# Local attention in a fused four-layer kernel: scores as four products of 32 partitions, keys zeroed four ways per chunk, rstd kept by token, units alternating between two pairs of PSUM banks

## The chip, the cores and the metric

The kernel runs on one NeuronCore of a Trainium2 chip. The metric is the device time in microseconds (us) of one execution. Matmuls of fp32 operands run as two records each in the trace; of fp32r operands as one.

## The reference, cut to what matters

The reference runs four layers over 2048 tokens of 128 channels (each an attention or scan part and a feed-forward part). The change touches the attention part of the second layer, L1:

```python
NUM_HEADS = 16; HEAD_DIM = 8; WINDOW = 64; SCALE = 8.0 / HEAD_DIM   # SCALE is 1
xw = x.reshape(B * nw, WINDOW, C)
qkv = (xw @ W_qkv).reshape(B * nw, WINDOW, 3, NUM_HEADS, HEAD_DIM)
q, k, v = (qkv[:, :, 0], qkv[:, :, 1], qkv[:, :, 2])
q = _layernorm(q, ln_gamma, ln_beta)        # over the 8 values of a head
k = _layernorm(k, ln_gamma, ln_beta)
attn = jnp.einsum('bqhd,bkhd->bhqk', q * SCALE, k)
attn = jax.nn.softmax(attn, axis=-1)
out = jnp.einsum('bhqk,bkhd->bqhd', attn, v).reshape(B * nw, WINDOW, C)
out = out @ W_proj + b_proj
```

## The kernel before, in words

The 2048 tokens are four chunks of 512 (`NC = 4`, `CH = 512`); a chunk is four tiles of 128. Each engine runs its own hand-written list of steps in order; semaphores tie the lists together. The stages follow each other over all chunks: a first stage, FFN0 (16 experts, 8 blocks a chunk), the local attention (`attn`), FFN1, a scan, FFN2, a linear attention, two dense blocks. While a stage works on chunk c, hooks (`attn_hooks`) prepare the normalised input of a later chunk or stage and add the result of the chunk before to the residual.

In the attention stage a chunk is eight units (`UN = 8`, 32 in all). Unit N is tile N // 2 and half of the heads, u = N % 2: eight heads, two windows of 64 tokens. Per unit: `scores` (L1219 to L1224) makes two products, one per window, of all 128 channels: 64 queries are loaded, 512 columns stream (8 heads x 64 keys); keys of one head must be zero in the channels of all others, so there is one masked copy of the keys per head. The result fills bank `G[u]`. DVE takes the maximum (L1395) and subtracts it into `PRB` (L1398); ACT takes the exponential in place (L1329); PE transposes four 128 x 128 blocks into bank `U[u]` (`turn`, L1232); ACT copies them to `PT` (`evac`, L1335); PE multiplies with the values (`weigh`, L1244); after every second unit DVE divides by the sums (`finish`, L1374, L1380), which must be done before the next tile's first `weigh`, as both use one bank.

The masked copies are made per tile, 16 of 128 x 128 (`attn_mask`, L1188 to L1204): 8 on DVE and 4 on POOL (L1203), 4 on ACT (L1201), in two buffers (`KM`).

During a chunk the q, k and v of the next are prepared in steps (`PREPARE_AT`, `attn_prepare_*`): step 0 and 1 are the products for q and k (three fp32r products of 512 columns, L731 to L733), their squares and copies (L1145, L1146); step 2 the means of the squares, 32 rows by 512 tokens (L1107, L1108), square root on ACT (L1149, between two table loads) and reciprocal on DVE (L1176); step 3 the values (L1155); step 4 spreads the reciprocals over the channels by products of 32 rows (L1119, L1125), and DVE multiplies (L1181) and applies gain and bias (L1185), for k and then q. For chunk 0 these steps lie in the last chunk of FFN0 (`attn_early_*`). The values are turned and placed in two halves (L1135, L1169). The output of a chunk is turned, copied, split and projected during the next one (`attn_turn_pe` L1296, `attn_out_act` L1308, `attn_project_*` L1302, L1313, L1319, L1321).

`body_start` makes PE, ACT, DVE and POOL wait, before the first masks and scores, for FFN0's last result (L926). POOL also converts weights (`work`, L2117, L2118).

## Time and profile before

| | |
|---|---|
| median of 3 runs | 897.65 us (897.23 to 898.66) |
| the profiled execution | 897.48 us, span 895.7 us |
| PE busy | 734.7 us (82%) |
| DVE busy | 675.6 us (75%) |
| ACT busy | 575.3 us (64%) |
| POOL busy | 394.1 us (44%) |
| mean granted PE clock | 0.911 |

Times in the trace count from the start of the span. [...]

### The profile page before, as it was taken

The numbers are of one execution on the slowest core, as the hardware profiler recorded it, in microseconds if no ns is written. First come the engines' busy times: TensorE is split into PE (matmuls) and PEld (weight loads), VectorE is DVE, ScalarE is ACT, GpSimd is POOL, SyncE is SP. The second block draws the span as 40 slices with busy tenths as digits, with TensorE's granted clock in tenths as the row PEclk, the third lists the DMA queues.
The fourth block names the chain that finished last, engine by engine and source line by source line (L and its number), as shares of the span: only waits on it lengthen the run. The fifth ranks groups of instructions, "written<-read, shape, count | busy, mean of one in ns | idle before, by whom it ended". The sixth has DMA issues, their size and how long they took to land. (4 is left out here: it accounts for less than half of the span.)

```text
span 895.7 us, 11019 instructions
## 1 busy us (share of the span) xinstructions
PE 734.7 (82%) x3306; PEld 467.0 (52%) x3306; DVE 675.6 (75%) x1615; ACT 575.3 (64%) x926; POOL 394.1 (44%) x427
## 2 busy tenths in 40 slices
PE   4778998779999889999678888867777767777787
PEld 3666765345545567777555666642232222222575
DVE  6685776798898748787756667769898788786785
ACT  4264664657474535565636667767899979777776
POOL 6638654634445015544248767634333332230330
PEclk9999998988696869999969999998999889789999
DMA  4200001000000000000000000000000000000001
GB/s 134 69 12 15 15 15 33 19 23 24 12 25 19 1 0 1 1 1 0 1 13 23 1 1 0 1 0 1 1 0 1 1 1 0 1 0 1 1 1 48
DMA packets 9610, 11.59 MB, mean 13 GB/s; under 512 B 720, under 2 KB 5712, under 8 KB 9552
## 3 DMA queue, kind: packets, MB, share of 16 engines
q1 hardware_dynamic: 9552, 10.89, 4.2%
q8 instruction: 27, 0.44, 0.2%
q14 instruction: 31, 0.25, 0.1%
HBM read 9.84 MB, written 1.05 MB: 12 GB/s over the span
## 5 line engine op out<-in xcount | busy, mean ns | idle before, releaser
L989 POOL TENSOR_TENSOR rbuf<-B,rbuf 128x512 fp32r<-128x512 f32 x126 | 164.2, 1307 | 101.8 <-ACT rbuf L921 101.0
L968 DVE TENSOR_TENSOR B<-B,spread_bank 128x512 f32<-128x512 f32 x128 | 87.1, 682 | 47.2 <-ACT B L913 33.0
L921 ACT ACTIVATE rbuf<-B 128x512 fp32r<-128x512 f32 x132 | 83.0, 628 | 49.0 <-PE y_bank L733 38.8
L497 POOL TENSOR_SCALAR small<-small 128x4 f32<-128x4 f32 x32 | 8.1, 252 | 175.9 <-DVE small L387 175.7
L731 PE MATMUL y_bank<-rbuf,WH 128*128 128x512 f32 x150 | 64.2, 428 | 20.8 <-POOL rbuf L989 14.4
L955 DVE TENSOR_TENSOR B<-B,up_banks 128x512 f32<-128x512 f32 x68 | 46.5, 684 | 45.4 <-PE up_banks L733 28.5
L911 ACT ACTIVATE B<-gate_banks 128x512 f32<-128x512 f32 x68 | 40.8, 599 | 61.6 <-PE gate_banks L733 60.4
L1715 ACT ACTIVATE B<-B,VEC 128x1024 f32<-128x1024 f32 x48 | 55.2, 1150 | 22.3 <-DVE B L1710 22.3
L731 PE MATMUL gate_banks<-XH,WH 128*128 128x512 f32 x152 | 66.7, 439 | 0.8 <-ACT YT L1313 0.8
L733 PE MATMUL gate_banks<-XH,WL 128*128 128x512 f32 x152 | 62.4, 411 | 0.0
L732 PE MATMUL gate_banks<-XL,WH 128*128 128x512 f32 x152 | 61.9, 407 | 0.0
L1203 POOL TENSOR_SCALAR B<-S,WR 128x128 f32<-128x128 f32 x64 | 39.2, 629 | 49.7 <-DVE S L1185 38.1
L733 PE MATMUL y_bank<-rbuf,WL 128*128 128x512 f32 x150 | 60.2, 402 | 0.0
L732 PE MATMUL y_bank<-rbuf,WH 128*128 128x512 f32 x150 | 60.0, 400 | 0.0
L1617 POOL TENSOR_SCALAR WH<-WK 128x512 fp32r<-128x512 f32 x22 | 13.8, 628 | 104.6 <-issue 57.9
L1244 PEld LDWEIGHTS spread_bank<-VB,B 128*128 128x128 f32 x256 | 37.6, 226 | 34.1 <-issue 26.2
L866 PE MATMUL spread_bank<-SCT,WE 128*128 128x512 f32 x96 | 42.6, 444 | 10.7 <-DVE B L968 8.7
L1716 ACT ACTIVATE B<-B 128x1024 f32<-128x1024 f32 x48 | 50.5, 1052 | 0.0
L913 ACT ACTIVATE B<-gate_banks,WR 128x512 f32<-128x512 f32 x64 | 43.8, 687 | 10.0 <-PE gate_banks L733 9.5
L731 PEld LDWEIGHTS y_bank<-rbuf,WH 128*128 128x128 f32 x150 | 28.9, 193 | 40.2 <-POOL rbuf L989 23.2
L1221 PE MATMUL gate_banks<-B,S 128*64 128x512 f32 x128 | 44.6, 786 | 5.3 <-issue 3.8
L1244 PE MATMUL spread_bank<-VB,B 128*128 128x36 f32 x256 | 41.1, 314 | 2.0 <-DVE Z L1380 2.0
(318 smaller groups left out, 2110.8 us busy)
## 6 DMA issues: line engine op xcount, KB each, us to landing
STG<-in_w_split SPq DMA_DIRECT2D x27, 256.0 KB, 2.7
X<-in_x SPq DMA_DIRECT2D x4, 256.0 KB, 4.6
out<-X SPq DMA_DIRECT2D x4, 256.0 KB, 2.3
WR<-in_w_raw SPq DMA_DIRECT2D x1, 524.5 KB, 4.0
STG<-in_w_exact SPq DMA_DIRECT2D x2, 256.0 KB, 2.7
STG<-in_w_split SPq DMA_DIRECT2D x5, 64.0 KB, 1.9
STG<-in_w_split SPq DMA_DIRECT2D x1, 192.0 KB, 2.3
STG<-in_w_split SPq DMA_DIRECT2D x1, 128.0 KB, 2.1
```

The costliest lines, as they stand in the source:

```text
L731: nc.tensor.matmul(dst, w[0], x[0], start=start, stop=False)
L732: nc.tensor.matmul(dst, w[0], x[1], start=False, stop=False)
L733: return nc.tensor.matmul(dst, w[1], x[0], start=False, stop=stop)
L913: nc.scalar.activation(AO[n % 2], G[n % 2][:, :], ACT.Relu, bias=raw("b1_2", b, 1))\
L921: nc.scalar.activation(rbuf[n % 2][:, :], HO[n % 3], ACT.Copy).then_inc(hh_ready, 1)
L955: nc.vector.tensor_tensor(MO[n % 2], AO[n % 2], U[n % 2][:, :], ALU.mult).then_inc(mul_done, 1)
L968: nc.vector.tensor_tensor(HO[n % 3], src, SP[:, :], ALU.mult).then_inc(h_ready, 1)
L989: e_.tensor_tensor(rbuf[2 + n % 2][:, :], HO[n % 3], rbuf[n % 2][:, :].bitcast(F32), ALU.subtract).then_inc(hl_ready, 1)
L1221: i = nc.tensor.matmul(G[u][w * WIN:(w + 1) * WIN, :], QN[c_ % 2][:, tok], KM[tile % 2][:, HU * u:HU * u + HU, w * WIN:(w + 1) * WIN], sta ...
L1244: i = nc.tensor.matmul(SP[:, pr * 36:(pr + 1) * 36], PT[u][:, q * P:(q + 1) * P], VB[:, tile % TL, pr, :, :, :].rearrange("p a b d -> p (a ...
L1715: nc.scalar.activation(CS[p % 4], AB[p % 4], ACT.Sin, scale=-TURN, bias=half_pi).then_inc(cos_ready, 1)
L1716: nc.scalar.activation(SN[p % 4], RB[p % 4], ACT.Sin, scale=-TURN).then_inc(sin_ready, 1)
```

## The change

Scores: each unit is now four products. The heads of a unit are four neighbours in one 32-partition group (`k` = 0, 1) and again four in the next; a product takes 32 partitions, 64 queries and 4 x 64 = 256 key columns, and writes 64 partitions of one of two banks (`SB2[u]`: the pair G for u = 0, the pair U for u = 1). Of keys only four copies a chunk are needed, head h mod 4 each, 128 x 512, with gain and bias applied in the same operation (`attn_keys`): two on ACT, two on POOL, none on DVE. The transposes of unit N go into the same pair of banks as its scores, so the scores of unit N + 2 wait for the copy (`evac`) of unit N, where they waited for the subtraction (L1398) before. On PE `weigh` comes before the scores, on ACT `evac` before the exponential, and `finish` one unit earlier on DVE.

Rstd by token: step 2 is eight products of 16 columns, with 128 tokens as rows; square root and reciprocal work on 128 x 128 instead of 32 x 512. ACT spreads them to 128 x 512 twice (`attn_spread_act`), and steps 4 and 5 turn them back on PE (four products of 128 columns each) into the routing bank, k and q at separate units. The first two units' scores are issued within FFN0's last blocks and `body_start` is gone; FFN0's last two down products now stand behind them on PE.

```diff
         def later_weights(g, chain):
+            for row, dst in (("ln_g1", key_g), ("ln_b1", key_b)):
+                i = nc.gpsimd.tensor_scalar(dst, raw("head_of_4"), raw(row), 1.0, ALU.mult, ALU.mult)
+            chain(i)
             WM32 = buf[11]
...
                 for at_ in lagged(f, c, b, f.lag):
                     down(*at_)
+                    if f is FFN0 and at_ == (NC - 1, f.blocks - 3):
+                        for N in range(2):
+                            attn_scores(pe, N)
...
+        KG = 4
         QN = [S0[:, 0:CH], S0[:, CH:2 * CH]]
-        KN = [S0[:, 2 * CH:3 * CH], S0[:, 3 * CH:4 * CH]]
         Zf = Z[:, :, :].rearrange("p a b -> p (a b)")
         AT = [Zf[:, 0:CH], Zf[:, CH:2 * CH]]
         qc, kc = Zf[:, 2 * CH:3 * CH], Zf[:, 3 * CH:4 * CH]
-        KM = [B[:, 4 * k_:4 * k_ + 4, :].rearrange("p a b -> p (a b)").rearrange("p (h t) -> p h t", h=NH)
-              for k_ in range(2)]
-        PRB = [buf[8], buf[9]]
-        PT = [buf[10], buf[11]]
+        KM = [B[:, 7:11, :], B[:, 3:7, :]]
+        PRB = [buf[0], buf[1]]
+        PT = [buf[2], buf[11]]
+        SB2 = [GG[:, :].rearrange("p (k x) -> p k x", k=2)[:, :, 0:KG * WIN],
+               UU[:, :].rearrange("p (k x) -> p k x", k=2)[:, :, 0:KG * WIN]]
         WK = sb("WK", [P, 3, CH])
         sqq, sqk = WK[:, 0, :], WK[:, 1, :]
-        sdev, rstd = WK[0:GR, 2, :], WK[0:GR, 0, :]
+        sdev, rstd = WK[:, 2, 0:TL * GR], WK[:, 2, TL * GR:2 * TL * GR]
         A32w = WK[:, 1, :]
...
-        PREPARE_AT = {1: 0, 2: 1, 3: 2, 5: 3}
+        PREPARE_AT = {0: (0,), 1: (1,), 2: (2,), 4: (4,), 5: (5, 3)}
+        EARLY_AT = {0: (0,), 1: (1,), 2: (2,), 4: (4,), 5: (5,), 6: (3,)}
...
+            if b == 3:
+                attn_spread_act(a, 0)
+            if b == 6:
+                attn_keys(nc.scalar, 0)
...
-                nc.tensor.matmul(R[0:GR, :], raw("mean_k"), sqk, start=True, stop=False)
-                nc.tensor.matmul(R[0:GR, :], raw("mean_q"), sqq, start=False, stop=True).then_inc(var_full, 1)
+                for j in range(TL):
+                    for sq, name, at_ in ((sqq, "mean_q", 0), (sqk, "mean_k", NH)):
+                        i = nc.tensor.matmul(R[:, j * GR + at_:j * GR + at_ + NH], sq[:, j * P:(j + 1) * P],
+                                             raw(name, at_, NH), start=True, stop=True)
+                i.then_inc(var_full, 1)
...
-            if step == 4:
-                if not c:
-                    pe.wait_ge(v_copied, 1)
-                pe.wait_ge(rstd_qk, c + 1)
-                nc.tensor.matmul(R[:, :], raw("spread_k")[0:GR, :], rstd, start=True, stop=True).then_inc(rstd_full, 1)
-            if step == (4 if c else 5):
-                if c:
-                    pe.wait_ge(v_copied, c + 1)
-                else:
-                    pe.wait_ge(qk_read, 1)
-                nc.tensor.matmul(VQ(c)[:, :], raw("spread_q")[0:GR, :], rstd, start=True, stop=True).then_inc(rstd_full, 1)
+            if step in (4, 5):
+                pe.wait_ge(rstd_wide, 2 * c + step - 3)
+                if step == 5:
+                    pe.wait_ge(qk_read, 2 * c + 1)
+                for j in range(TL):
+                    i = nc.tensor.matmul(R[:, j * P:(j + 1) * P], (sqq, QN[c % 2])[step - 4][:, j * P:(j + 1) * P],
+                                         ident, start=True, stop=True)
+                i.then_inc(rstd_full, 1)
...
+        def attn_spread_act(a, c):
+
+            a.wait_ge(rstd_qk, c + 1)
+            if c >= 2:
+                a.wait_ge(s_full, UN * (c - 1))
+            for dst, at_ in ((sqq, NH), (QN[c % 2], 0)):
+                nc.scalar.activation(dst.rearrange("p (t h d) -> p t h d", t=TL, d=HD),
+                                     bcast(rstd.rearrange("p (t h) -> p t h", t=TL)[:, :, at_:at_ + NH].unsqueeze(3),
+                                           [P, TL, NH, HD]), ACT.Copy).then_inc(rstd_wide, 1)
...
-            if step == 4:
-                for k, (bank_, x, dst) in enumerate(((R, kc, KN), (VQ(c), qc, QN))):
-                    v.wait_ge(rstd_full, 2 * c + k + 1)
-                    v.wait_ge(centred, 2 * c + 2)
-                    nc.vector.tensor_tensor(x, x, bank_[:, :], ALU.mult).then_inc(qk_read, 1)
-                    v.wait_ge(qk_read, 2 * c + k + 1)
-                    if c >= 2:
-                        v.wait_ge(s_full, UN * (c - 1))
-                    nc.vector.tensor_scalar(dst[c % 2], x, raw("ln_g1"), raw("ln_b1"), ALU.mult, ALU.add)\
-                        .then_inc(qk_ready, 1)
-
-        def attn_mask(eng, tile):
-
-            c, i_ = tile // TL, tile % TL
-            if tile >= NC * TL:
+            if step in (4, 5):
+                k, x = step - 4, (kc, qc)[step - 4]
+                v.wait_ge(rstd_full, 2 * c + k + 1)
+                v.wait_ge(centred, 2 * c + 2)
+                nc.vector.tensor_tensor(x, x, R[:, :], ALU.mult).then_inc(qk_read, 1)
+            if step == 5:
+                v.wait_ge(qk_read, 2 * c + 2)
+                if c >= 2:
+                    v.wait_ge(s_full, UN * (c - 1))
+                nc.vector.tensor_scalar(QN[c % 2], qc, raw("ln_g1"), raw("ln_b1"), ALU.mult, ALU.add)\
+                    .then_inc(qk_ready, 1)
+
+        def attn_keys(eng, c):
+            if c >= NC:
                 return
-            heads, done = {nc.vector: (range(0, 8), masked_dve), nc.gpsimd: (range(8, 12), masked_pool),
-                           nc.scalar: (range(12, 16), masked_act)}[eng]
-            eng.wait_ge(qk_ready, 2 * c + 1)
-            if tile >= 2:
-                eng.wait_ge(s_full, 2 * (tile - 2) + (1 if eng is nc.vector else 2))
-            for h in heads:
-                dst, src = KM[tile % 2][:, h, :], KN[c % 2][:, i_ * P:(i_ + 1) * P]
+            eng.wait_ge(qk_read, 2 * c + 1)
+            if c >= 2:
+                eng.wait_ge(s_full, UN * (c - 1))
+            elif c == 1:
+                eng.wait_ge(yt_ready, count(2, 0))
+            for j in ((0, 1) if eng is nc.scalar else (2, 3)):
+                dst = KM[c % 2][:, j, :]
                 if eng is nc.scalar:
-                    i = eng.activation(dst, src, ACT.Copy, scale=raw("head_mask", h, 1))
+                    i = eng.activation(dst, kc, ACT.Identity, scale=key_g[:, j:j + 1], bias=key_b[:, j:j + 1])
                 else:
-                    i = eng.tensor_scalar(dst, src, raw("head_mask", h, 1), None, ALU.mult)
-            i.then_inc(done, 1)
+                    i = eng.tensor_scalar(dst, kc, key_g[:, j:j + 1], key_b[:, j:j + 1], ALU.mult, ALU.add)
+            i.then_inc(keys_act if eng is nc.scalar else keys_pool, 1)
+
+        def attn_scores(pe, N):
+            if N >= NU:
+                return
+            u, c, i_ = N % 2, N // UN, N % UN // 2
+            if N % UN == 0:
+                pe.wait_ge(keys_act, c + 1)
+                pe.wait_ge(keys_pool, c + 1)
+                pe.wait_ge(qk_ready, c + 1)
+            if N >= 2:
+                pe.wait_ge(pt_ready, N - 1)
+            else:
+                pe.wait_ge(act_done, NC * FFN0.blocks)
+                pe.wait_ge(mul_done, NC * FFN0.blocks)
+            for w in range(2):
+                tok = slice(i_ * P + w * WIN, i_ * P + (w + 1) * WIN)
+                for k in range(2):
+                    rows = slice(32 * (2 * u + k), 32 * (2 * u + k) + 32)
+                    i = nc.tensor.matmul(SB2[u][w * WIN:(w + 1) * WIN, k, :], QN[c % 2][rows, tok],
+                                         KM[c % 2][rows, :, tok], start=True, stop=True)
+            i.then_inc(s_full, 1)
...
                 if N:
                     turn(N - 1)
-                scores(N + 1)
                 if N >= 2:
                     weigh(N - 2)
+                if N:
+                    attn_scores(pe, N + 1)
                 if n == 0:
                     attn_values_pe(pe, c, 1)
                     if c == 0:
                         hook(-1)
+                if nxt:
+                    for step in PREPARE_AT.get(n, ()):
+                        if step != 3:
+                            attn_prepare_pe(pe, c + 1, step)
                 if n == 3 and c:
                     attn_turn_pe(pe, c - 1)
                 if n == 4 and c:
                     attn_project_pe(pe, c - 1)
-                attn_hooks(n, c, hook, 4)
-                if n in PREPARE_AT and nxt:
-                    attn_prepare_pe(pe, c + 1, PREPARE_AT[n])
+                attn_hooks(n, c, hook, 5)
+                if nxt and n == 5:
+                    attn_prepare_pe(pe, c + 1, 3)
...
-            if c + 1 < NC:
-                pe.wait_ge(qk_read, 2 * c + 4)
+            if c + 2 < NC:
+                pe.wait_ge(centred, 2 * c + 5)
...
                 if N >= 2:
                     a.wait_ge(o_full, N - 1)
-                nc.scalar.activation(PT[N % 2], U[N % 2][:, :], ACT.Copy).then_inc(pt_ready, 1)
-
-            if c == 0:
-                body_start(a, 2, 0)
-                attn_mask(nc.scalar, 0)
+                else:
+                    a.wait_ge(h_ready, NC * FFN0.blocks)
+                nc.scalar.activation(PT[N % 2].rearrange("p (k x) -> p k x", k=2), SB2[N % 2], ACT.Copy)\
+                    .then_inc(pt_ready, 1)
+
             for n in range(UN):
                 N = c * UN + n
-                probs(N)
                 if N:
                     evac(N - 1)
-                if n == 1:
+                probs(N)
+                if n == 0:
                     attn_values_act(a, c, 1)
+                if nxt:
+                    for step in PREPARE_AT.get(n, ()):
+                        if step != 3:
+                            attn_prepare_act(a, c + 1, step)
+                if n == 3 and nxt:
+                    attn_spread_act(a, c + 1)
+                if n == 3 and c:
+                    attn_out_act(a, c - 1)
                 if n == 4 and c:
                     attn_project_act(a, c - 1)
                 attn_hooks(n, c, hook, 5)
-                if n in PREPARE_AT and nxt:
-                    attn_prepare_act(a, c + 1, PREPARE_AT[n])
-                if n == 3 and c:
-                    attn_out_act(a, c - 1)
-                if n % 2 == 0:
-                    attn_mask(nc.scalar, c * TL + n // 2 + 1)
+                if n == 5 and nxt:
+                    attn_keys(nc.scalar, c + 1)
+                if n == 6 and nxt:
+                    attn_prepare_act(a, c + 1, 3)
...
-                Sv = G[u][:, :].rearrange("p (h k) -> p h k", k=WIN)
-                chain(nc.vector.tensor_reduce(amax[:, HU * u:HU * u + HU], Sv, AX.X, ALU.max))
+                Sv = SB2[u].rearrange("p k (h x) -> p k h x", x=WIN)
+                amax_ = amax[:, HU * u:HU * u + HU].rearrange("p (k h) -> p k h", k=2)
+                chain(nc.vector.tensor_reduce(amax_, Sv, AX.X, ALU.max))
                 if N >= 2:
                     v.wait_ge(p_turned, N - 1)
-                nc.vector.tensor_tensor(PRB[u].rearrange("p (h k) -> p h k", k=WIN), Sv,
-                                        bcast(amax[:, HU * u:HU * u + HU].unsqueeze(2), [P, HU, WIN]), ALU.subtract)\
-                    .then_inc(s_read, 1)
-                if n == 6 and nxt:
+                nc.vector.tensor_tensor(PRB[u].rearrange("p (k h x) -> p k h x", k=2, x=WIN), Sv,
+                                        bcast(amax_.unsqueeze(3), [P, 2, KG, WIN]), ALU.subtract).then_inc(s_read, 1)
+                if nxt and n == 3:
+                    attn_prepare_dve(v, c + 1, 2)
+                if nxt and n == 4:
                     attn_prepare_dve(v, c + 1, 4)
-                if u == 0:
-                    if N >= 4:
-                        finish(N // 2 - 2)
-                    attn_mask(nc.vector, N // 2 + 1)
+                if nxt and n == 5:
+                    attn_prepare_dve(v, c + 1, 5)
                 if n == 4 and c:
                     attn_project_dve(v, c - 1)
                 if n == 0 and c == 0:
                     hook(-1)
-                attn_hooks(n, c, hook, 7)
-                if n == 5 and nxt:
-                    attn_prepare_dve(v, c + 1, 2)
+                attn_hooks(n, c, hook, 6)
+                if u == 1 and N >= 3:
+                    finish(N // 2 - 1)
...
-                body_start(g, 2, 0)
-                attn_mask(nc.gpsimd, 0)
+                attn_keys(nc.gpsimd, 0)
             for n in range(UN):
-                if n % 2 == 0:
-                    attn_mask(nc.gpsimd, c * TL + n // 2 + 1)
+                if n == 5:
+                    attn_keys(nc.gpsimd, c + 1)
                 attn_hooks(n, c, hook, 4)
                 if n % 2 and n > 1:
                     work()
```

## Rows read from the trace of the kernel before

**Rows 1.** The page: its first line.
```profile
span 895.7 us, 11019 instructions
```

**Rows 2.** Windows, a chunk each: us, busy PE, PEld, DVE, ACT, POOL, granted clock, DMA.
```profile
163.80:197.10 33.30, 27.01 (x130) 13.46 (x127) 31.78 (x80) 20.40 (x49) 17.40 (x28) 0.91 0.09 24
197.10:236.80 39.70, 38.81 (x169) 22.23 (x169) 33.95 (x94) 24.19 (x62) 16.76 (x24) 0.76 0.08 21
236.80:274.10 37.30, 36.14 (x169) 20.63 (x169) 34.87 (x94) 23.72 (x61) 16.61 (x24) 0.82 0.07 18
274.10:321.30 47.20, 38.23 (x199) 26.14 (x199) 32.20 (x116) 22.36 (x56) 7.77 (x12) 0.75 0.02 7
```

**Rows 3.** Timeline of PE in chunk 2: start, us, operation.
```profile
247.09 1.08 PE L1221 MATMUL gate_banks<-B,S 128*64 128x512 f32 x4
248.10 1.08 PE L1244 MATMUL spread_bank<-VB,B 128*128 128x36 f32 x8
249.01 0.48 PE L731 MATMUL route_bank<-XH,WH 128*128 128x512 f32 x1
...
249.80 0.60 PE L1232 MATMUL up_banks<-WR,B 128*128 128x128 f32 x4
```

**Rows 4.** The same, 22 us later.
```profile
271.02 1.09 PE L1232 MATMUL up_banks<-WR,B 128*128 128x128 f32 x4
272.08 1.98 PE L1221 MATMUL gate_banks<-B,S 128*64 128x512 f32 x4
```

**Rows 5.** Groups of instructions, 163.8 to 321.3 us: count, busy us, mean ns, idle before.
```profile
L1203 POOL TENSOR_SCALAR B<-S,WR 128x128 f32<-128x128 f32 x60 | 36.5, 625 | 44.0 <-DVE S L1185 38.1 <-PE gate_banks L1221 5.9
L1203 DVE TENSOR_SCALAR B<-S,WR 128x128 f32<-128x128 f32 x120 | 30.8, 333 | 0.4
...
L1395 DVE TENSOR_REDUCE small<-gate_banks 128x8 f32<-128x512 f32 x32 | 21.8, 682 | 11.5 <-PE gate_banks L1221 11.1
L1329 ACT ACTIVATE B<-B 128x512 f32<-128x512 f32 x32 | 20.1, 629 | 32.2 <-DVE B L1398 31.8
L1201 ACT ACTIVATE B<-S,WR 128x128 f32<-128x128 f32 x60 | 19.0, 390 | 0.0
L1335 ACT ACTIVATE B<-up_banks 128x512 f32<-128x512 f32 x32 | 18.8, 586 | 8.2 <-PE up_banks L1232 8.1
...
L1380 DVE TENSOR_TENSOR Z<-spread_bank,small 64x64 f32<-64x64 f32 x64 | 11.4, 218 | 0.8
L1176 DVE RECIPROCAL WK<-WK 32x512 f32<-32x512 f32 x3 | 10.0, 3330 | 0.0
L1374 DVE RECIPROCAL small<-spread_bank 64x16 f32<-64x16 f32 x32 | 8.1, 252 | 5.3 <-PE spread_bank L1244 5.1
L1169 ACT ACTIVATE VB<-route_bank 64x64 f32<-64x64 f32 x56 | 7.8, 218 | 10.4 <-PE route_bank L1135 6.9 <-PE spread_bank L1244 3.5
...
L2117 POOL TENSOR_SCALAR WH<-STG 128x512 fp32r<-128x512 f32 x9 | 5.6, 621 | 0.0
...
L1149 ACT ACT_TABLE_LOAD x3 | 3.8, 1283 | 0.1
...
L1185 DVE TENSOR_SCALAR S<-Z,WR 128x512 f32<-128x512 f32 x6 | 3.3, 547 | 0.2
...
L1308 ACT ACTIVATE WK<-y_bank 128x512 f32<-128x512 f32 x4 | 2.3, 582 | 5.9 <-PE y_bank L1296 5.9
```

**Rows 6.** Timeline, the step from FFN0 to attention.
```profile
154.43 0.46 POOL L2118 TENSOR_TENSOR WL<-STG,WH 128x128 fp32r<-128x128 f32 x1
...
158.00 0.60 PE L1135 MATMUL route_bank<-WR,KVT 128*128 128x128 f32 x4
...
162.41 3.07 PE L1221 MATMUL gate_banks<-B,S 128*64 128x512 f32 x8 [3.82 <-issue]
...
165.27 0.63 ACT L1329 ACTIVATE B<-B 128x512 f32<-128x512 f32 x1 [2.19 <-DVE B L1398]
```

**Rows 7.** The chain that ended last, in the linear attention: start, us, what.
```profile
782.05 0.99 PE spread_bank L1656 x8
```

More of the change, by code:

```diff
@@ L1087, in attn_early_dve @@
                 attn_prepare_dve(v, 0, 2)
-            if b == 6:
-                attn_prepare_dve(v, 0, 4)
+            for step in (4, 5):
+                if step in EARLY_AT.get(b, ()):
+                    attn_prepare_dve(v, 0, step)
         def attn_prepare_pe(pe, c, step):
@@ L1143, in attn_prepare_act @@
                 if c and step == 0:
[L1144 removed]
+                    a.wait_ge(qk_ready, c)
+                if c and step == 1:
+                    a.wait_ge(keys_pool, c)
                 nc.scalar.activation(sq, src[:, :], ACT.Square)
```

56 lines of the change are left out of this document (16 added, 40 removed).

## The prediction

> **What bounds it now.** I read the windows by chunk first. The span is 895.7 us [rows 1]; the attention stage, from the first maximum to FFN1's first product, is the four stretches of [rows 2], 157.5 us. In chunks 1 and 2 PE is busy for 38.81 of 39.70 and 36.14 of 37.30 us, DVE for 33.95 and 34.87: PE carries the chunk and DVE is close behind. ACT (24 us) and POOL (17 us) have room. The timeline of PE gives the second half of the answer. At the high clock the scores of a unit take 1.01 us start to start, weighing 0.91, one fp32r triple 0.79, and four transposes about 0.55 [rows 3]. In the same chunk, 22 us later, the same transposes last 1.09 and the same scores 1.98 [rows 4]: the clock is at its lower level. The mean clocks of 0.76 and 0.82 [rows 2] say how long: (1 - 0.76) x 2 x 39.7 = 19 us of chunk 1, 13 us of chunk 2. PE's work at the high clock is 8 x (0.55 + 1.01 + 0.91) = 19.8, four triples 3.2, and some 6 us of means, spreads and turns: 29 us. Half of 13 us on top makes 35.5 of the 37.3. So a chunk costs PE's work, the half-clock stretch, and one or two us of waits. DVE's masks and its reciprocal of 3.33 us are what PE waits for when it waits [rows 5].
>
> **The change, part by part.**
> *Masks.* 120 operations of DVE (30.8 us), 60 of POOL (36.5) and 60 of ACT (19.0) go [rows 5]. What comes per chunk is two operations of 128x512 on ACT (the nearest row is the copy, 0.58) and two on POOL (0.62) [rows 5]. One gain-and-bias operation of DVE (0.55) goes too. DVE loses about 8 us a chunk, ACT nets 5 - 1.2.
> *Rstd.* The reciprocal streams 128 columns instead of 512. Between 3330 ns for 512 and 252 ns for 16 [rows 5], a line gives 0.95 us: -2.4 on DVE. ACT gains two spreads of 128x512, 1.2 us. On PE the means become 16 records; weighing has 8 of such loads in 0.91 [rows 3], so 1.8 us, and the turns of steps 4 and 5 are 0.9 each: together 3.6, as before.
> *Scores.* No row shows products of different partition groups side by side. Upper bound: they share the array only by window, as now; then 256 columns twice cost the present 1.01. Lower bound: all four overlap. Four products of 512 columns in four column groups take 0.99 [rows 7], so half the columns take 0.5. I take 0.55, since that row is the nearest in kind (four small tiles at once). PE saves 0.45 a unit, 3.7 a chunk; with 1.01 it would save nothing.
> [...]
>
> *New waits.* This is the dear part. Scores of unit N + 2 now stand behind `evac` of N, and ACT does much else. I lay out chunk 1 at the high clock, 0 being the end of its first scores; durations as above, exp 0.63, evac 0.59, a DVE pass 0.69 [rows 5], placing values 8 x 0.14 = 1.1 (the row's 218 ns are overlapped ends).
> - Scores 2 end at 3.0: PE has turned and weighed at 2.0, but ACT places values and only then copies.
> - Scores 3 at 7.0: placing and the squares and copies of q (2.2 us on ACT) hold evac to 6.4.
> - Scores 4 at 10.2: the k product and its square and copy.
> - Scores 5 at 14.0: PE does the means (1.8), then transposes and weighs.
> - Scores 6 at 18.6: ACT waits for the means, changes tables twice (1.28 each, [rows 5]), does the exponential, waits for the reciprocal, spreads twice, copies the output (0.58) and the next input, and reaches evac at 17.4. PE is idle for 1.5 us.
> - Scores 7 at 24.1: DVE stands before step 4 until PE has issued it behind scores 6 (19.5), then multiplies, splits the output and the input (2 us), and only at 22.4 takes the next maximum. The projection waits for the split, 1.9 us of PE.
> - Scores 8 at 29.1: step 5, the tail's turn and the v product are 2.2 us of PE; DVE's multiply, gain and `finish` (0.5 + 0.8) hold weighing to 27.6.
> - The next chunk's first scores at 31.9.
> PE's work is 25.4 us of these 31.9. The chain scores, two DVE passes, exp, turn, evac alone is 4.2 us for two units, so it does not bind; the side work on ACT and DVE does.
>
> *The clock.* Before the fall in chunk 2 PE was busy but partly with products that fill a quarter of the array (means, spreads: 32 rows or columns). The spreads now fill it, but scores fill it for half the time, and the stretch from scores 4 to scores 7 has 3 to 4 us of idle PE. I therefore keep a half-clock stretch of about 14 us a chunk, over the scores 4 to 7. There PE's share is 8 to 9 us of high-clock work, of which most is on the path: +7.5 a chunk. [...]
>
> *The sum.* Chunks 1 and 2: 31.9 + 7.5 = 39.4 each, against 39.7 and 37.3. Chunk 0 has no output of a chunk before it: 29.1 + 5.5 = 34.6 against 33.3. The last chunk has no preparation; the same layout gives 33.2 from its first scores to FFN1's first product, +7 for the clock, 40.2 against 47.2 [rows 2], because PE no longer waits for masks there.
> *Start.* Masks and scores stood between the last value turn at 158.0 and the first exponential at 165.27 [rows 6]. Now the scores are done inside FFN0's end, but they need POOL's two key copies, and POOL is busy until 154.9 [rows 6]: 156.2, so they hold FFN0's last two down products by about 1.5 us, and with these the values and ACT's result. The exponential follows at some 163: it counts as a start at 160.8 instead of 163.8, -3.
> In FFN0's last chunk DVE saves the same 2.4 us of reciprocal; -1.5 of it reaches PE (0 to -2.4), ACT's extra 2.4 us lie in its idle time.
> Total: -3 - 1.5 + 1.3 - 0.3 + 2.1 - 7.0 = -8.4 us. The profiled execution took 897.48 for its span of 895.7, 0.17 below the median of 897.65; 897.5 - 8.4 = **889.1**. SP's queue keeps its order, and POOL, which loses 36.5 us of masks, has the weights ready earlier: 0.
>
> **The rivals.**
> *A: the clock stays high.* For it: less waiting for masks, and steps 4 and 5 fill the array. Then the 27.5 us of clock cost in my sum go: -36; with half of them gone, -22, **875**. Against it: each of the first three chunks lost the clock in its second half [rows 2, 4] though PE was busy there.
> *B: the half-clock stretch grows (slower).* The loop scores, evac, scores keeps PE waiting in every slot, and short 32-row scores keep the array emptier. If the stretch goes from 14 to 28 us in each chunk, PE's 25 us of work lie almost wholly in it: +7.5 in three chunks and about +3 in the last, 889.1 + 25 = **914**. It decides from where the clock costs 9 instead of the 7 us a chunk of my sum, which is only some 4 us more at the low level; a mild form, +12 us, gives 901. By itself, scores at 1.01 would add some 8 us where PE is on the path: 897.
> *C: no change.* The expected gain is only in the last chunk and at the start; if the layout is 2 us too short per chunk it is gone: **897.5**. That the change does not do what it says I exclude: the masks leave the lists.
>
> **How the numbers follow.** A measurement of this kernel tells about 0.2%, 1.8 us, from no change. My forecast (a gain of 2 to 16 us) gets 0.43, A 0.24, B 0.25, C 0.08. Faster 0.67, same 0.08, slower 0.25. The likeliest case alone spans 881 to 896. Reaching half into A and into the mild form of B, the range is 868 to 905: the clock term is the unknown that makes it this wide.
>
> **What would show it.** Right: no L1203 or L1201; DVE busy 22 to 25 us a chunk; a reciprocal near 0.95; scores of a unit in about 0.55 start to start; chunk 0 near 34, chunks 1 and 2 near 39, and the last near 40 us; DVE idle for about 4 us ahead of step 4; ACT as the releaser of scores in the first slots; a mean clock near 0.8 in each chunk. Wrong: a mean clock over 0.9 (A) or under 0.65 (B), scores at 1.0, or chunks under 33 us at the present clock, which would mean that ACT and DVE get through their side work without holding the loop.

## The result: 914.5 us, slower, and the profile after

The changed kernel takes 914.52 us (median of 4 runs, 909.35 to 918.38), the kernel before, on the same chip, 898.15 (897.23 to 898.83): a ratio of 1.0186, 95% interval 1.0154 to 1.0218. The forecast was 889.1 with a range of 868 to 905; rival B gave 914. Medians here and below are of all executions; three of the four of late_swap_fill ran at 929.3 to 930.3 us and one at 914.93, and one of rstd_mask_7 ran at 930.29 and one of true_64 at 901.39, over 1.5% above the fastest of their kernel; the ratios leave these slow ones out.

The windows by chunk of the changed kernel, beside [rows 2] (first maximum of the chunk to that of the next; the last ends at FFN1's first product; columns as there: length, busy time of PE, its loads, DVE, ACT and POOL, then the granted clock):

```profile
158.10:198.80 40.70, 36.36 (x200) 29.00 (x198) 21.64 (x53) 21.86 (x47) 7.73 (x10) 0.63 0.08 20
198.80:243.70 44.90, 39.14 (x230) 31.98 (x229) 24.23 (x62) 21.44 (x49) 9.52 (x10) 0.64 0.07 18
243.70:290.10 46.40, 39.77 (x222) 32.30 (x221) 24.17 (x62) 21.53 (x48) 9.50 (x10) 0.63 0.05 15
290.10:340.10 50.00, 42.79 (x219) 35.08 (x217) 25.69 (x86) 18.19 (x42) 3.08 (x4) 0.53 0.02 6
```

DVE fell from 34 to 24 us a chunk as forecast, and the chunks still grew, from 39.7 and 37.3 to 44.9 and 46.4 us. Cut into windows of 0.5 us, the trace shows two levels of the granted clock: from 150 to 345 us 296 of 390 windows read 0.50 and 79 read 1.00, the other 15 lie between (in the kernel before, from 150 to 325 us, 139 of 350 read 0.50, 197 read 1.00 and 14 lie between). So the clock is at the lower level for (1 - 0.64) x 2 x 44.9 = 32 us of chunk 1 and 34 of chunk 2, against 19 and 13 before. PE's busy time rose, from 38.8 and 36.1 to 39.1 and 39.8 us, though its work shrank, because the work is stretched by the clock (weighing a unit lasts 0.98 us at the high clock and 1.76 at half clock, below). Nearly all of the loss lies in this stage: FFN1's first product starts at 340.07 against 321.28, and what follows takes 576.3 us against 574.4.

The groups of the changed operations (158 to 340 us; line, engine, names, shapes, count, then busy time and mean ns, then idle time ahead of them):

```profile
L1250 PE MATMUL gate_banks<-B,S 32*64 32x256 f32 x123 | 16.4, 610 | 9.1 <-ACT B L1367 9.0
...
L1124 PE MATMUL route_bank<-WR,WK 128*128 128x16 f32 x48 | 8.0, 312 | 0.0
...
L1230 POOL TENSOR_SCALAR B<-Z,small 128x512 f32<-128x512 f32 x6 | 6.6, 1111 | 61.0 <-DVE Z L1208 61.0
...
L1228 ACT ACTIVATE B<-Z,small 128x512 f32<-128x512 f32 x6 | 4.5, 801 | 0.0
...
L1208 DVE TENSOR_TENSOR Z<-Z,route_bank 128x512 f32<-128x512 f32 x6 | 4.1, 688 | 25.6 <-PE route_bank L1138 25.6
...
L1203 DVE RECIPROCAL WK<-WK 128x128 f32<-128x128 f32 x3 | 2.9, 953 | 4.6 <-ACT WK L1166 4.6
```

The reciprocal takes 0.953 us (forecast 0.95); DVE idles 25.6 us in six ahead of steps 4 and 5, 4.3 each (forecast 4, for step 4); ACT's `evac` is what scores wait for, 9.0 us in the even units. The keys were dearer: 0.80 us each on ACT and 1.11 on POOL, for which I had taken a copy's 0.58 and 0.62.

PE's timeline around the chunk's start, the one longer stretch at the high clock (238.3 to 252.0 us; start, duration from first start to last end, and in brackets the idle time before):

```profile
241.35 0.98 PE L1272 MATMUL spread_bank<-VB,B 128*128 128x36 f32 x8
242.41 0.66 PE L1250 MATMUL gate_banks<-B,S 32*64 32x256 f32 x8
243.00 0.66 PE L1150 MATMUL route_bank<-WR,KVT 128*128 128x128 f32 x4
...
247.71 0.98 PE L1272 MATMUL spread_bank<-VB,B 128*128 128x36 f32 x8
251.59 0.82 PE L1250 MATMUL gate_banks<-B,S 32*64 32x256 f32 x8 [2.90 <-ACT B L1367]
252.34 0.80 PE L736 MATMUL route_bank<-XH,WH 128*128 128x512 f32 x1
...
254.63 1.76 PE L1272 MATMUL spread_bank<-VB,B 128*128 128x36 f32 x8
```

A unit's scores take 243.00 - 242.41 = 0.59 us from start to start (forecast 0.55; the duration of 0.66 runs 0.07 past the next start), where the same number of products of all 128 rows takes 1.02 (rows_128, from 263.58 to 264.60), and four products of 128 columns on all rows and columns, with half as many columns in all, take 0.99 (rows_128, L1138, from 280.01 to 281.00): four products of different row and column groups do run side by side. Weighing is 0.98 before 252.0 and 1.76 after it; the granted clock is 1.00 from 238.3 to 252.0 and 0.50 from 252.0 to 266.0. The clock falls here right behind a wait of 2.90 us, in which PE's third scores stand behind `evac`, and ACT places values before it.

The head of the stage, which was to gain 3 us (PE, then ACT and POOL):

```profile
151.17 0.50 PE L871 MATMUL spread_bank<-SCT,WE 128*128 128x512 f32 x1 [2.74 <-DVE B L976]
...
156.89 0.70 PE L1250 MATMUL gate_banks<-B,S 32*64 32x256 f32 x4 [3.83 <-issue]
...
158.07 0.80 PE L736 MATMUL y_bank<-rbuf,WH 128*128 128x512 f32 x1
...
160.80 1.05 PE L1150 MATMUL route_bank<-WR,KVT 128*128 128x128 f32 x4
...
147.80 1.51 ACT L1228 ACTIVATE B<-Z,small 128x512 f32<-128x512 f32 x2
149.21 0.59 ACT L919 ACTIVATE B<-gate_banks 128x512 f32<-128x512 f32 x1
...
165.04 0.63 ACT L1359 ACTIVATE B<-B 128x512 f32<-128x512 f32 x1
...
155.28 1.51 POOL L1230 TENSOR_SCALAR B<-Z,small 128x512 f32<-128x512 f32 x2
```

ACT copies keys ahead of FFN0's last silu (L919), and PE waits 2.74 us (1.35 in late_scores, where the copies stand behind it, though the product itself starts no earlier there, at 151.18); then it waits 3.83 us for POOL's keys inside FFN0, in front of the last two down products, which start at 158.07 at half clock (0.80). The first exponential is at 165.04, before it was at 165.27 [rows 6].

### The profile page after: what moved, and what is told of

The parts are those of the page before. It is cut to its first block and busy times, and to the rows that moved or that the text cites. A ratio compares the mean times of both kernels' runs of the same rounds, so it can differ in the third digit from the quotient of the medians.

```text
span 916.4 us, 11149 instructions
## 1 busy us (share of the span) xinstructions
PE 750.6 (82%) x3530; PEld 514.4 (56%) x3530; DVE 636.3 (69%) x1483; ACT 565.1 (62%) x878; POOL 365.2 (40%) x373
## 5 line engine op out<-in xcount | busy, mean ns | idle before, releaser
L963 DVE TENSOR_TENSOR B<-B,up_banks 128x512 f32<-128x512 f32 x68 | 46.5, 684 | 46.0 <-PE up_banks L738 25.4
L919 ACT ACTIVATE B<-gate_banks 128x512 f32<-128x512 f32 x68 | 40.6, 598 | 59.5 <-PE gate_banks L738 58.3
L736 PEld LDWEIGHTS y_bank<-rbuf,WH 128*128 128x128 f32 x150 | 29.1, 194 | 43.4 <-POOL rbuf L997 23.8
L1272 PEld LDWEIGHTS spread_bank<-VB,B 128*128 128x128 f32 x256 | 50.9, 295 | 3.3 <-issue 1.8
L1272 PE MATMUL spread_bank<-VB,B 128*128 128x36 f32 x256 | 49.7, 358 | 2.3 <-DVE Z L1416 2.2
L2149 POOL TENSOR_TENSOR WL<-STG,WH 128x512 fp32r<-128x512 f32 (+3 forms) x34 | 40.8, 1200 | 2.8
L1729 DVE TENSOR_SCALAR B<-gate_banks 128x1024 f32<-128x1024 f32 x32 | 38.9, 1215 | 2.2 <-PE gate_banks L1671 1.2
```

The costliest lines, as they stand in the source:

```text
L736: nc.tensor.matmul(dst, w[0], x[0], start=start, stop=False)
L963: nc.vector.tensor_tensor(MO[n % 2], AO[n % 2], U[n % 2][:, :], ALU.mult).then_inc(mul_done, 1)
L1272: i = nc.tensor.matmul(SP[:, pr * 36:(pr + 1) * 36], PT[u][:, q * P:(q + 1) * P], VB[:, tile % TL, pr, :, :, :].rearrange("p a b d -> p (a ...
```

## The experiments

All are measured against the kernel before on the same chip in the same job; each job had its own median of before, 898.1 to 899.5. The four lengths run from the first maximum of a chunk to that of the next, the last to the last maximum. Half clock is (1 - clock) x 2 x length, summed over the four, in the one execution of each kernel that was profiled (for late_swap_fill there is no interval). rows_128, rows_64 and before_rows_32 compute another attention than the reference.

| kernel | median us | ratio to before, 95% | chunks 0, 1, 2, 3 | half clock of all |
|---|---|---|---|---|
| before | 898.15 | 1 | 33.3, 39.7, 37.3, 33.3 | 50 of 144 |
| after | 914.52 | 1.0154 to 1.0218 | 40.7, 44.9, 46.4, 35.5 | 129 of 167 |
| fill_after | 917.59 | 1.0154 to 1.0268 | 46.0, 42.5, 45.4, 37.8 | 93 of 172 |
| rows_128 | 915.12 | 1.0114 to 1.0231 | 44.4, 46.5, 38.8, 34.0 | 69 of 164 |
| late_scores | 909.86 | 1.0068 to 1.0201 | 35.7, 49.5, 43.6, 30.6 | 111 of 159 |
| fill_before | 896.54 | 0.9949 to 1.0023 | 34.7, 40.9, 40.8, 34.1 | 38 of 150 |
| late_fill | 921.03 | 1.0210 to 1.0334 | 37.5, 49.9, 53.2, 40.2 | 86 of 181 |
| late_swap | 905.22 | 1.0042 to 1.0107 | 35.5, 44.4, 44.2, 35.2 | 120 of 159 |
| late_swap_fill | 929.53 | - | - | - |
| rstd_alone | 895.01 | 0.9936 to 0.9993 | 32.6, 38.9, 37.5, 35.8 | 40 of 145 |
| rows_64 | 891.31 | 0.9897 to 0.9945 | 31.8, 41.5, 37.1, 31.4 | 77 of 142 |
| before_rows_32 | 937.77 | 1.0401 to 1.0476 | 36.9, 48.6, 48.6, 43.5 | 143 of 178 |
| scores_alone | 909.73 | 1.0067 to 1.0156 | 38.4, 44.2, 44.0, 31.9 | 115 of 158 |
| rstd_mask_7 | 922.57 | 1.0176 to 1.0312 | 42.1, 38.6, 49.7, 33.2 | 77 of 164 |
| true_64 | 898.01 | 0.9947 to 1.0005 | 34.3, 42.5, 40.8, 34.2 | 99 of 152 |
| true_64_order | 892.64 | 0.9923 to 0.9963 | 38.8, 38.1, 37.6, 31.7 | 89 of 146 |

### Does the clock cost the time? Fillers and fuller products

```diff
# fill_after, in turn (before its wait for the exponential) and after an even unit's weighing
+        def fill(n, dst):
+            for _ in range(n):
+                nc.tensor.matmul(dst, wh("wqk1c")[0], WH[:, 0:224], start=True, stop=True)
...
+                pe.wait_ge(s_read, N + 1)
+                fill(4 if N else 12, SB2[u][:, 0, 0:224])
                 pe.wait_ge(p_ready, N + 1)
...
+                if u == 0:
+                    fill(4, SP[:, 288:CH])
```

> The changed kernel with idle-time products of TensorE added in the attention stage: four of 128x224 (fp32r, nothing reads them) while TensorE waits for each unit's exponential, four after every even unit's weighing, 24 in the wait for POOL's keys at FFN0's end. They add about 45 us of busy time at half clock, half of it at the high clock. Theory T (the changed kernel is slow because its emptier array loses the high clock for nearly the whole stage): the clock stays high in most of the stage, the chunks come near the 32 us of my layout, and the time falls by 15 to 35 us to 880 to 900. Rival R (scores behind evac and the side work on ACT and DVE set the chunks whatever the clock): the clock may rise, but the time stays within 4 us of 914 or goes above it.

The fillers raised the clock only in part (93 of 172 us at half clock, from 129 of 167), and each costs PE 0.13 us at the high and 0.25 us at half clock (four take 0.53 us from 204.92 to 205.45 and 0.98 from 182.95 to 183.93); in the timeline PE mostly goes from them to its next work with no idle time between, so that they lay on the path. The time is the one that R named and not T's, but with the fillers on the path it doesn't tell the two apart. (24 more fillers stand ahead of the first scores.) fill_before puts the same fillers into the units of the kernel before:

> The kernel before with the same idle-time products: four of 128x224 ahead of each unit's turn while the exponential is awaited, four after every even unit's weighing. Its attention stage has 62 us at half clock in 157.5. Theory T: most of that goes, the chunks are bound by VectorE's 34 us and by waits, 880 to 892. If the clock were worth little there (R): 897 to 905, the added products on the path.

No clear difference from before, and neither T's 880 to 892 nor quite R's 897 to 905. That clock gained and fillers paid cancel is my reading, not shown apart. late_fill and late_swap_fill, with more of them, were worse than the kernels that they were added to (late_swap_fill's best execution, 914.93, is above all of late_swap's), and T's numbers for them were wrong; late_fill's 921.0 is the case of a clock that stays low, 915 to 925, which decides nothing:

> late_scores with more idle-time products: six of 128x224 while each exponential is awaited, eight after every even unit's weighing, twelve ahead of the third scores, eight ahead of each projection. The first filled kernel kept half clock for 30.7 us of chunk 0 and for 93 of 172 us in all, and its fillers lay on the path there. Theory T: late_scores is at 909.9; if the clock now stays high for over two thirds of the stage, the chunks take about 33.5 us plus 2 to 3 us of fillers (that is what the chunks of the changed kernel and of late_scores give when their half-clock time is taken out at 0.37 us each), and the time is 888 to 900. Rival R: over 905 although the clock is high. If the clock stays low the run decides nothing: 915 to 925.

> late_fill and late_swap together. Theory T: at the high clock waits are what is left, so that the order gains 3 to 5 us on late_fill, 885 to 896. Rival R: no better than late_swap.

In late_fill chunk 2 the clock stayed low for 31 of 53 us although PE was busy for 49.2: fillers at half clock did not bring it back for some 30 us and lengthened the chunk.

```diff
# rows_128
-                    i = nc.tensor.matmul(SB2[u][w * WIN:(w + 1) * WIN, k, :], QN[c % 2][rows, tok],
-                                         KM[c % 2][rows, :, tok], start=True, stop=True)
+                    i = nc.tensor.matmul(SB2[u][w * WIN:(w + 1) * WIN, k, :], QN[c % 2][:, tok],
+                                         KM[c % 2][:, :, tok], start=True, stop=True)
```

> The changed kernel, its score products taking all 128 rows instead of 32; nothing else differs (64 columns, 256 streamed). A product then sums the keys of four row groups, so the attention that it computes is another; the number of instructions and their order are the same. TensorE's scores should take 1.0 instead of 0.55 us a unit at the high clock, since products of all rows overlap only by column group. Theory T: the fuller array keeps the high clock in more of the stage, so that the kernel is FASTER with twice the time in its score products: 890 to 908. Rival R: 0.45 us a unit more on the path of at least half of the 32 units, 920 to 930.

Chunks 1 and 2 of rows_128 have the same instructions:

```profile
203.38:249.89 46.51, 39.45 (x225) 30.96 (x224) 24.28 (x61) 21.56 (x48) 9.52 (x10) 0.74 0.06 18
249.89:288.66 38.77, 30.57 (x226) 23.96 (x225) 24.23 (x62) 21.23 (x48) 9.54 (x10) 0.96 0.06 18
```

The scores' time nearly doubled (0.43 us x 32 = 14 us) and the median did not move beyond the noise, 915.1 against 914.5: the half-clock time fell. The traces overstate by how much, 129 to 69 us, since they show the slowest execution of the changed kernel (918.38) and the fastest of rows_128 (908.58); at the medians the mean clocks are 0.872 and 0.895. T's 890 to 908, a faster kernel, did not come, and the median is under R's 920 to 930. And the pair shows the price: 7.74 us for 24.2 - 3.1 = 21.1 us more at half clock, 0.37 us each.

### The same length, another filling

These two change how many rows of the array a product covers and neither its time nor any order. They also change the values that are multiplied, to which the text comes back below.

```diff
# rows_64, on late_swap
-                    rows = slice(32 * (2 * u + k), 32 * (2 * u + k) + 32)
+                    rows = slice(64 * k, 64 * k + 64)
# before_rows_32, on the kernel before
-                    i = nc.tensor.matmul(G[u][w * WIN:(w + 1) * WIN, :], QN[c_ % 2][:, tok],
-                                         KM[tile % 2][:, HU * u:HU * u + HU, w * WIN:(w + 1) * WIN],
+                    i = nc.tensor.matmul(G[u][w * WIN:(w + 1) * WIN, :], QN[c_ % 2][32:64, tok],
+                                         KM[tile % 2][32:64, HU * u:HU * u + HU, w * WIN:(w + 1) * WIN],
```

> late_swap with each score product taking 64 rows instead of 32 (rows 0 to 63 and 64 to 127, 64 columns each); number, length and order of the products are the same, and the four still take places of the array of their own. Each head's scores then sum two row groups, so the attention that it computes is another. The scores should take the same 0.55 to 0.6 us a unit. Theory T (the clock follows how full the array is): more of the stage at the high clock than in late_swap, which had 121 of 159 us at half clock, and 3 to 12 us faster than its 905: 893 to 902. Rival R (the clock follows only the gaps, or is not what costs): within 2 us of 905.

> The kernel before with its score products taking rows 32 to 63 instead of all 128; 64 columns, 512 streamed, order and waits stay. A score then sums a quarter of the masked keys' rows, so the attention that it computes is another. The scores should still take 1.01 us a unit at the high clock. Theory T: an emptier array loses the clock: half-clock time in the stage from 62 us to over 90, and slower than before by 8 to 20 us: 906 to 918. Rival R: within 2 us of 898. In between if VectorE, not TensorE, carries the chunks of the kernel before.

Both go T's way, and beyond its ranges: rows_64 is 13.9 us faster than late_swap, before_rows_32 is 39 us slower than before, twice the upper end of what T asked for. Chunk 2 of late_swap, then of rows_64:

```profile
237.51:281.70 44.19, 39.56 (x226) 32.36 (x225) 24.08 (x62) 21.46 (x48) 8.91 (x10) 0.62 0.05 15
```

```profile
228.55:265.68 37.13, 32.67 (x226) 26.70 (x225) 23.99 (x61) 21.43 (x48) 9.02 (x10) 0.78 0.06 18
```

The scores' own durations (count, then min/median/max ns), first of rows_64, then of before_rows_32:

```profile
L1246 PE MATMUL gate_banks<-B,S x128: 376/631/687, 154.6 to 291.8; 64*64 64x256 f32 x128
```

```profile
L1221 PE MATMUL gate_banks<-B,S x128: 587/1056/1112, 162.4 to 340.7; 32*64 32x512 f32 x128
```

The least of before_rows_32, 587 ns, is that of a product of 512 columns at the high clock (592 in the kernel before, with 128 rows); the median, 1056, is now that of the low one (before: median 643, most 1116). Its windows, chunks 1 and 2:

```profile
201.25:249.81 48.56, 47.67 (x169) 27.15 (x169) 34.21 (x94) 23.90 (x61) 16.53 (x24) 0.61 0.06 17
249.81:298.37 48.56, 47.67 (x169) 27.25 (x169) 34.10 (x94) 24.08 (x61) 16.46 (x24) 0.61 0.05 14
```

PE is busy for 98% of these chunks and still at half clock for 38 of 48.6 us: what lowers the clock here is hardly a gap (the longest is 0.84 us).

How far rows and how far values do it is not fully separated. In before_rows_32 the keys of 12 of the 16 heads are zero in the rows that are left; in rows_64 each streamed column has 16 rows that are not zero, in late_swap 8. true_64 (below) takes 64 rows with 8 that are not zero, and is 7.2 us faster than late_swap, with 99 us at half clock against 120, though it has more work on DVE and GpSimd: rows count at equal values. The rest of rows_64's gain can be its values, or the key copies that true_64 adds.

### Which part of the change?

```diff
# rstd_alone, on the kernel before (the change's step 2, spreads and turns, masks and scores as before)
-        sdev, rstd = WK[0:GR, 2, :], WK[0:GR, 0, :]
+        sdev, rstd = WK[:, 2, 0:TL * GR], WK[:, 2, TL * GR:2 * TL * GR]
...
# scores_alone, on late_swap: the same lines undone
```

> The kernel before with the change's token-major rstd alone: reciprocal of 128 columns on VectorE, two spreads on ScalarE, 16 short mean products and eight turns on TensorE in place of two and two products of 512 columns. Masks and scores stay. VectorE loses 2.4 us of 34 a chunk, TensorE's work stays near 3.6 us at the high clock. Theory T: the mean products stream 16 columns for each load and empty the array for 2 us, but the spreads then fill it; the stage's half-clock time stays within 10 us of 62: 894 to 899. If this part carried a good share of the loss: 902 or more. Without either: VectorE binds only part of the chunk, -1 us a chunk.

> late_swap with the old rstd: means in two products of 512 columns, reciprocal of 512 columns (3.3 us) on VectorE at the fourth unit, two spreads of 32 rows on TensorE; no spreads on ScalarE. It holds the change's scores, keys and twin banks alone. Theory T: the scores part carries the loss of the clock; the time stays at 903 to 912 though TensorE's mean products shrink from 3.6 us at half clock to about 2. Rival: the short mean products of token-major rstd (16 of 16 columns) are what empties the array; then the clock rises and the time is 890 to 898. The longer reciprocal may cost 1 to 2 us a chunk.

The rstd alone is a small gain (895.0, ratio 0.9936 to 0.9993). The scores with keys and twin banks are the loss: 909.7 with the old rstd, 905.2 with the new, whose intervals overlap. The short mean products, which I had under suspicion, are not it. Chunk 2 of rstd_alone was nearly free of half clock:

```profile
233.65:271.19 37.54, 31.31 (x194) 20.71 (x194) 32.88 (x95) 24.57 (x63) 16.69 (x24) 0.95 0.07 19
```

37.5 us at 0.95, where before had 37.3 at 0.82 [rows 2]: 10 us less at half clock, and no shorter. Between rstd_alone's own chunks 1 and 2 (38.9 and 37.5 us) 7.1 us of half clock go with 1.4 us, 0.19 each. So in the old layout the first ten or so microseconds at half clock seem to cost little; that DVE's 33 us and its order carry the chunk there is my inference. Beyond that they cost much, as rstd_mask_7 shows, which moves one of DVE's masks to ACT and lets the scores of even units wait for ACT's masks too:

```diff
-            heads, done = {nc.vector: (range(0, 8), masked_dve), nc.gpsimd: (range(8, 12), masked_pool),
-                           nc.scalar: (range(12, 16), masked_act)}[eng]
+            heads, done = {nc.vector: (range(0, 7), masked_dve), nc.gpsimd: (range(8, 12), masked_pool),
+                           nc.scalar: ((7, *range(12, 16)), masked_act)}[eng]
```

> rstd_alone (the kernel before with the token-major rstd) with one of VectorE's eight masks of a tile moved to ScalarE (0.26 against 0.32 us each), for which scores of even units then wait too. In rstd_alone chunk 2 took 37.5 us at a mean clock of 0.95 with VectorE busy 32.9. If VectorE carries it there: 1 us a chunk off, 889 to 894. If the wait on ScalarE's masks, which come late in the slot, takes its place: 895 to 900.

```profile
202.69:241.31 38.62, 32.70 (x193) 22.07 (x193) 32.10 (x91) 25.91 (x68) 16.56 (x24) 0.90 0.08 21
241.31:291.00 49.69, 43.86 (x193) 30.13 (x193) 31.17 (x91) 25.95 (x68) 16.82 (x24) 0.67 0.05 14
```

Neither expectation held: by the ratios (1.0244 and 0.9965) it is some 25 us slower than rstd_alone. One of two chunks with the same instructions took 38.6 us, the other 49.7, with 7.7 and 32.8 us at half clock, 0.44 us each. What in it tips the clock wasn't tried.

### The start and the order

```diff
# late_scores
-                    if f is FFN0 and at_ == (NC - 1, f.blocks - 3):
-                        for N in range(2):
-                            attn_scores(pe, N)
...
+            if c == 0:
+                for N in range(2):
+                    attn_scores(pe, N)
...
-            if b == 6:
-                attn_keys(nc.scalar, 0)
             if b == 7:
+                attn_keys(nc.scalar, 0)
# late_swap, on late_scores: attn_prepare_dve(v, c + 1, 4) of n == 4 behind attn_project_dve(v, c - 1)
```

> The changed kernel with the first two units' scores moved out of FFN0's end to the head of the attention stage, and ACT's two key copies of chunk 0 moved behind its last silu. Theory S (the early scores hold FFN0's last two down products behind POOL's keys and put them at half clock): 2 to 4 us faster, 910 to 912. Theory T alone: within 2 us of 914, because scores then follow the keys at the same time and the gap of TensorE is only elsewhere. If the chunks' half-clock stretch depends on the clock at the start, it may gain more than 4.

> late_scores with one order changed on VectorE: the split of the output (for the projection) ahead of its multiply of step 4, for which it waits some 4 us. TensorE waited 2.4 us for this split in each of two chunks. Rival R: 3 to 6 us faster than late_scores, 904 to 907. Theory T: at half clock TensorE's work carries the chunk and the shorter wait is partly filled by work; 1 to 4 us, 906 to 909.

ACT's timeline of late_scores has the first exponential here:

```profile
159.60 0.63 ACT L1358 ACTIVATE B<-B 128x512 f32<-128x512 f32 x1
```

That is 5.4 us earlier than in the changed kernel, and the median fell by 4.7 (909.9), a little more than S had asked for. The order on VectorE gave another 4.6 (905.2), within R's 904 to 907 and more than T's 906 to 909. Neither step is clear of the noise by itself (the intervals of neighbours overlap); together they are, 9.3 us: waits are a real part of the loss. 7 us above before are left, with chunks 1 and 2 at a clock of 0.62. Neither run touches the waits of scores for `evac`, 9.7 us in four times in late_swap.

### A version that beats both

```diff
# true_64, on late_swap
+            for j in (range(4, 8) if eng is nc.gpsimd else range(4)):
+                dst, src = KM[half][:, j, :], kc[:, half * 256:half * 256 + 256]
...
+                    rows = slice(64 * k, 64 * k + 64)
+                    at_ = i_ % 2 * P + w * WIN
+                    i = nc.tensor.matmul(SB2[u][w * WIN:(w + 1) * WIN, k, :], QN[c % 2][rows, tok],
+                                         KM[N // 4 % 2][rows, KG * u:KG * u + KG, at_:at_ + WIN], start=True, stop=True)
...
-                    pr = 4 * u + q
+                    pr = 4 * (q // 2) + 2 * u + q % 2
# true_64_order, in attn_act
-                if n == 0:
+                if n == 1:
                     attn_values_act(a, c, 1)
```

> The fuller array with the reference's own result: late_swap, with keys zeroed by place in eight instead of four, so that a score product can take 64 rows of eight heads and stream four of their zeroed copies (256 columns). A unit then holds heads 4u to 4u+3 and 8+4u to 8+4u+3, and weighing follows that order. Keys are made for half a chunk at a time, since eight copies of a chunk don't fit twice: eight operations of 128x256 a half, by ScalarE and GpSimd for the first half, by VectorE and GpSimd for the second. PE's instructions are those of rows_64, which took 891.3. Theory T: 889 to 896, faster than both kernels; the copies are 1 to 2 us more a chunk on GpSimd and VectorE, which have room. Rival R (what rows_64 gained came from its data or is lost to the added copies): 898 or more.

> true_64 with ScalarE's placing of the second half of the values moved from the first slot of a chunk to the second, behind the copy of the transposed probabilities for which TensorE's third scores of the chunk wait (2.9 us in each of two chunks of rows_64). Theory: 1 to 1.5 us a chunk, less where the k product behind the placed values comes later: 3 to 6 us faster than true_64. Rival (the k product and all its steps shift by as much): within 1 us.

true_64 is 7.2 us below late_swap but 6.7 above rows_64, whose PE instructions it has: T's direction, not its 889 to 896, at the lower edge of R's "898 or more", and level with before. Its DVE and GpSimd are busier by 1.7 and 2.8 us a chunk than in rows_64, its clock is at half for 99 us, not 77. How these hang together was not taken apart. Moving the placing of values then took off 5.4 us (its interval and true_64's overlap slightly), and the longest wait of scores for `evac` went from 2.9 us to 1.0 (a part came back: the k product now waits for the placed values, 5.4 us in three times). Chunks 1 and 2:

```profile
197.63:235.77 38.14, 34.90 (x226) 28.68 (x225) 25.68 (x65) 21.87 (x50) 11.83 (x16) 0.72 0.08 22
235.77:273.33 37.56, 34.52 (x226) 28.18 (x225) 25.80 (x66) 21.98 (x50) 11.84 (x16) 0.73 0.06 18
```

892.64 us, ratio 0.9943 (0.9923 to 0.9963): the lowest median here of a kernel that computes the reference, faster than before and after; from rstd_alone (895.0) the noise does not separate it.

## Why the prediction was wrong

- **The clock term failed.** The step that failed was "I therefore keep a half-clock stretch of about 14 us a chunk". It was 32 and 34 us in chunks 1 and 2, 30 in chunk 0 and 47 up to FFN1. I had weighed the idle time and that "scores fill it for half the time", and priced neither. rows_64 and before_rows_32 show that what the score products cover and multiply, at equal times and order, moves the time by -14 and +39 us, and true_64 that the rows count by themselves. Four products of 32 rows, 64 columns and 256 streamed do a quarter of the array work of two of 128 rows, 64 columns and 512 streamed, and the high clock hung on it in good part. Not in whole: rows_128 has that work back and still has more half clock than before (69 against 50 us) and no lower median than the changed kernel.
- **The high-clock layout was nearly right, by an estimate.** Take the price of 0.37 us from rows_128 (late_scores gives the same: 49.45 - 43.59 = 5.86 us for 42.5 - 27.0 = 15.5). Chunk 1 would be 44.9 - 0.37 x 32 = 33.1 us at the high clock, chunk 2 33.8; the layout had 31.9. The price in the sum, 7.5 / 14 = 0.54 a microsecond, was too high, the length of the stretch too small by more.
- **Where the 29 us went.** The profiled execution, the slowest of the four, took 918.38. Counting its start 1.47 us ahead of the first exponential, as before, chunk 0 took 35.2 us (forecast 34.6), chunks 1 and 2 44.9 and 46.4 (39.4), the last 50.0 (40.2): 22.9 us. The start and FFN0's end give 163.6 against the 159.3 forecast, 4.3; FFN1 and on 1.9. Together 29.1 of 918.4 - 889.1 = 29.3.
- **The start term failed.** "The exponential follows at some 163", with POOL's keys done at 156.2: they were done at 156.8, but the product behind them ran at half clock, and ACT's key copies, which "lie in its idle time", stood ahead of a silu. The last down product before that wait started its last record at 152.66, against 155.06 in the kernel before, so more than the 1.5 us that the sum gave FFN0's end was there; the wait took it. What I costed at nothing was queued in front of FFN0's own chain.
- **The steps that held**: reciprocal 0.953, scores 0.59 at the high clock, spreads 0.61 each, DVE's idle time ahead of steps 4 and 5, ACT as releaser of scores. The mean products take 3.6 us at half clock (1.96 in rows_128 at the high one; forecast 1.8).
- **Rival B** named the mechanism, the stretch, the emptier array and, by its sum, 914. I gave it 0.25, because I read the falls of before as given and not as set by the work in them. That its 914 meets the median of 914.5 is partly luck: its stretch was 28 us a chunk (30 to 34, and 47 in the last), its price 0.54 (0.37), and it had nothing for the start. Of B's two reasons the emptier array is shown (against late_swap, rows_64 is 13.9 us faster with 43 us less at half clock, true_64 7.2 us with 21 less). The waits of the loop, scores behind `evac`, are only partly tested: the fall at 252 stands right behind such a wait, and in true_64_order, where these waits shrank, 5.4 us and 10 us of half clock went; no run takes them out of the changed kernel. The 9.3 us of late_scores and late_swap are other waits. Rival A was out for the same reason as the forecast.
- **The old chunks were read wrongly too.** I took half of every half-clock microsecond of before as a loss. rstd_alone chunk 2 suggests that the first 10 or so cost little. By an estimate (its 37.5 us against the 33.1 and 33.8 above) what the change set free on DVE was worth up to some 4 us a chunk, but only at the high clock.

## What to carry over

Before making a product smaller to save TensorE's time, see in the trace whether the stage already loses the high clock in places, and count the rows that its products cover as well as their time (only rows were varied here). A product that can take more rows at the same duration can be worth extra copies on engines with room, as true_64 was against late_swap. Work pulled ahead into another stage's end has a queue in front of it on each engine that it touches; look at what is next behind it (here FFN0's last two down products, behind 3.83 us of PE's wait for POOL's keys).

## What the runs showed that I had not expected

- The granted clock falls while PE is busy 98% of the time, when the score products cover a quarter of the rows they did, which also drops most of the keys that aren't zero (before_rows_32: half clock for 38 of 48.6 us a chunk, from 19 and 13).
- Chunks of the same instructions in one execution differ by 11 us (rstd_mask_7: 38.6 and 49.7), and whole executions of the changed kernel by 9 us, 909.35 at a mean clock of 0.881 and 918.38 at 0.865.
- Products of 128x224 put into the wait for an exponential were not free: in fill_after's chunk 0 PE mostly had work waiting behind them (46.0 us, PE busy 43.3).
- A unit's score products of 64x64 take as long as those of 32x64: eight records in 0.66 us at the high clock and 1.13 at half clock, in rows_64 as in the changed kernel.
